# Eight images through a convolution–attention–experts block: the next image's first normalisation moved beside the experts, small products and evictions re-placed

## The reference, cut to what matters

```python
x  = group_norm(hidden, pre_g, pre_b) + pos_emb               # the "first normalisation"
sw = sigmoid(conv1x1(silu(conv3x3(silu(conv1x1(x))))))        # c1, c2, c3
sh = group_norm(x, norm_g, norm_b).transpose                  # tokens; q, k, v of 8 heads of 16
standard_out = softmax(q k^T / 4) v
multi_out = two 64-wide attentions, queries from (x * sw), keys and values from sh
x  = group_norm(ff(concat(standard_out, multi_out))) + hidden
t  = tokens(x)
t += attention(layernorm(t))                                  # 8 heads of 16
t += top-2-of-8 experts(layernorm(t))                         # 128 -> 512 -> 128, exact gelu
```

## Time and profile before

| | us |
|---|---|
| median of 3 runs (lowest, highest) | 3018.26 (3012.58, 3019.98) |
| profiled execution, its own time | 3020.56 |
| its span | 3018.8 |
| PE busy / DVE / ACT / POOL in the span | 2588.5 / 2057.8 / 1783.0 / 657.9 |
| mean granted TensorE clock | 0.95 of 2.4 GHz |
| one pass of the loop (first activation after the experts, L1313, 661.0 to 2769.8 for 7) | 351.5 |

### The profile page before, as it was taken

How to read it: one execution, slowest core, us unless ns; L and a number is a source line. 1 busy time by engine, 2 the same in 40 slices (tenths; PEclk the granted TensorE clock), 3 DMA queues, 4 the chain that set the end, 5 groups by cost and what they waited for, 6 DMA issues and landing times. The chain is left out here.

```text
span 3018.8 us, 42335 instructions
## 1 busy us (share of the span) xinstructions
PE 2588.5 (86%) x15054; PEld 1029.8 (34%) x15061; DVE 2057.8 (68%) x3120; ACT 1783.0 (59%) x3502; POOL 657.9 (22%) x611
## 2 busy tenths in 40 slices
PE   3796899988989899998999889898999989998844
PEld 1122222362225322262223522253222722235234
DVE  4756878477875878667785768758786677857520
ACT  1562577556765577556775567655775567755713
POOL 4000122015120240203320151202402043202123
PEclk9997899999999999999999989999999989999957
DMA  4002220274014530164202740145301632037034
GB/s 115 2 1 49 53 33 14 88 187 75 8 52 134 115 71 1 57 193 84 38 15 92 183 77 5 57 132 111 71 1 57 198 83 34 16 99 177 11 99 137
DMA packets 171978, 228.25 MB, mean 76 GB/s; under 512 B 29680, under 2 KB 101520, under 8 KB 171664
## 3 DMA queue, kind: packets, MB, share of 16 engines
q1 hardware_dynamic: 163600, 208.90, 28.4%
q0 software_dynamic: 8192, 16.79, 2.0%
HBM read 173.39 MB, written 51.31 MB: 74 GB/s over the span
## 5 line engine op out<-in xcount | busy, mean ns | idle before, releaser
L1433 DVE TENSOR_REDUCE blockmax<-ps 128x2 f32<-128x1024 f32 x1152 | 1355.0, 1220 | 380.1 <-PE ps L787 317.2
L1249 ACT ACTIVATE prob<-ps 128x512 f32<-128x512 f32 x2048 | 1110.7, 596 | 464.9 <-PE ps L964 453.2
L964 PE MATMUL ps<-qs,ks 99*128 99x512 bf16 x2048 | 687.2, 396 | 110.6 <-ACT prob L1249 48.5
L964 PEld LDWEIGHTS ps<-qs,ks 99*128 99x128 bf16 x2048 | 177.8, 99 | 775.0 <-ACT prob L1249 641.7
L624 POOL TENSOR_TENSOR rs<-vn,vec 128x1 f32<-128x1 f32 (+1 forms) x40 | 40.2, 1005 | 1475.1 <-DVE vn L1378 1051.2
L1297 ACT ACTIVATE prob<-ps,b1t 128x128 f32<-128x128 f32 x736 | 209.7, 368 | 169.3 <-PE ps L1080 169.3
L980 PE MATMUL ps<-prob,va_b 128*32 128x512 f32 x1984 | 283.8, 646 | 1.1 <-ACT oatt L1241 1.1
L980 PE MATMUL ps<-prob,va_a 128*32 128x512 f32 x2048 | 275.7, 610 | 3.0 <-ACT oatt L1241 1.7
L1275 ACT ACTIVATE prob<-ps 128x1024 f32<-128x1024 f32 x128 | 130.2, 1023 | 160.3 <-PE ps L1037 92.8
L675 POOL DMA_INDIRECT x_dram<-ta,slot_u x128 | 124.6, 973 | 313.5 <-DVE slot_u L1653 276.9
L1033 PE MATMUL ps<-routed,km 64*128 64x512 f32 x512 | 146.8, 651 | 12.6 <-DMA mrow<-maxrow 12.6
(11 more groups left out here) (247 smaller groups left out, 3182.6 us busy)
## 6 DMA issues: line engine op xcount, KB each, us to landing
parts_dram<-parts SPq DMA_DIRECT2D x32, 768.0 KB, 4.3
ks<-parts_dram SPq DMA_DIRECT2D x192, 128.0 KB, 4.4
qs<-parts_dram SPq DMA_DIRECT2D x384, 64.0 KB, 4.4
shared<-in_w SPq DMA_DIRECT2D x96, 256.0 KB, 3.4
prob<-in_w SPq DMA_DIRECT2D x96, 256.0 KB, 3.3
routed<-in_w SPq DMA_DIRECT2D x80, 256.0 KB, 3.5
xe<-in_w SPq DMA_DIRECT2D x48, 256.0 KB, 3.4
oatt<-in_w SPq DMA_DIRECT2D x48, 256.0 KB, 3.2
```

Of the source, the lines that this page charges most:

```text
L964: pe.matmul(ps[:, SC + h % 2, :], ks[:, slot_of(a, g), h, t * P:(t + 1) * P], qs[:, slot_of(a, g), q, h, :], start=True, stop=True).then_i ...
L1249: act.activation(prob[:, n % 3, h, :], ps[:, SC + h % 2, :], ACT.Exp, scale=HD ** -0.5).then_inc(exp_done[a], 1)
L1433: dve.tensor_reduce(cells, banks, AX.X, ALU.max).then_inc(blocks_used[f], 1)
```

## The change

- `pre` moves from token step 1 to expert slot 16, between pairs 5 and 6; `start_pre` to slot 8 on DVE; `load_next` from fetch 18 to fetch 11 on SP. x1 = ca * xin + cb is now made by ACT in halves in slots 18 and 19 (`scale_x`), and POOL adds the positions (`add_positions`).
- Token steps: start_x1 1 (was 3), start_x2 2 (5), norm 3 (6), start_xh 5 (7), normalisation in two halves at step 6 (8), kA0 6, kA1 7, qA0 8, qA1 9 (were 9, 10, 11, 13), vA 10, 11 (14, 15), vm 13, 14 (18, 19), c10 and c11 stay at 16, 17, c2 25 (24).
- ACT reads a small product of step n-1 in the middle of step n (between exponentials 1 and 2), in both windows, where it read that of step n at its end.
- The early pairs: one after `hidden`, one after `expert_out` in each slot from 13 on (were 1 in slot 13, 3 in slot 14, then 2 together behind `expert_out`).
- `third_part_b` moves from DVE to POOL; q's remainder goes to `tb`, so q no longer waits for k's third part. ACT's small products of a slot come before `second_part_b`.
- POOL's second reciprocal root stands behind 4 gathers instead of 12. On SP `spread_max("b", 2)` stands ahead of `spread_parts(0, 0)`.

```diff
-TOKEN_WINDOW = {1: ["pre"], 4: ["turn_b_1"], 6: ["norm"], 9: ["kA0"], 10: ["kA1"], 11: ["qA0"], 12: ["turn_b_2"],
-                13: ["qA1"], 14: ["vA0"], 15: ["vA1"], 16: ["c10"], 17: ["c11"], 18: ["vm0"], 19: ["vm1"],
-                20: ["turn_b_3"], 21: ["res0"], 22: ["res1"], 24: ["c2"], 26: ["c30"], 27: ["c31"],
+TOKEN_WINDOW = {3: ["norm"], 4: ["turn_b_1"], 6: ["kA0"], 7: ["kA1"], 8: ["qA0"], 9: ["qA1"], 10: ["vA0"],
+                11: ["vA1"], 12: ["turn_b_2"], 13: ["vm0"], 14: ["vm1"], 16: ["c10"], 17: ["c11"],
+                20: ["turn_b_3"], 21: ["res0"], 22: ["res1"], 25: ["c2"], 26: ["c30"], 27: ["c31"],
                 28: ["turn_a0_0"]}
-TOKEN_EXTRA = {0: ["start_pre"], 2: ["start_x0"], 3: ["start_x1"], 5: ["start_x2"], 7: ["start_xh"]}
+TOKEN_EXTRA = {1: ["start_x1"], 2: ["start_x2"], 5: ["start_xh"]}
-TURN_PAIR = UNIT
-BETWEEN_PAIRS = {2: "tg4", 9: "tg5", TURN_PAIR: "turn_b_0"}
+TURN_PAIR = UNIT + 1
+BETWEEN_PAIRS = {2: "tg4", 5: "pre", 8: "tg5", TURN_PAIR: "turn_b_0"}
+COEFS_PAIR = 8
+SCALE_SLOTS = (18, 19)
...
+def early_items(s, place):
+
+    d = SLOT_PAIRS * (s - PAIR_SLOT) + place
+    if s < PAIR_SLOT:
+        return []
+    return [x for x in (BETWEEN_PAIRS.get(d - 1), d) if x is not None]
...
-        rem = ta
+        rems = (ta, tb)
...
             if front:
+                if token:
+                    spread_max("b", 2)
                 spread_parts(0, 0)
                 spread_group(0, 0, 0)
-                if token:
-                    spread_max("b", 2)
...
-                        if token and front and (k, t) == (1, NT // 2):
+                        if token and front and (k, t) == (0, NT // 2):
                             rstd("norm_rstd", 1)
...
+            def add_positions():
+
+                for h in range(2):
+                    pool.wait_ge(done["x_scaled"], h + 1)
+                    pool.tensor_tensor(x1[:, cols(h)], x1[:, cols(h)], posw[:, cols(h)], ALU.add).then_inc(done["x1"], 1)
...
                     if experts and 1 <= s <= TILES:
                         hidden(s - 1)
+                    if token:
+                        for item in early_items(s, 0):
+                            early_item(item)
                     if experts and 2 <= s <= TILES + 1:
                         expert_out(s - 2)
...
+                    if token:
+                        for item in early_items(s, 1):
+                            early_item(item)
...
-                        exps(1, n)
+                        exps(1, n, 0)
+                    if token and front and n == 6:
+                        normalize(0)
+                    for name in small.token.get(n - 1, ()):
+                        small_product(name)
+                    if token:
+                        exps(1, n, 1)
+                    if token and front and n == 6:
+                        normalize(1)
...
-                    if i == 1:
-                        dve.wait_ge(done["k3_a"], h + 1)
-                    dve.tensor_tensor(rem[:, cols(h)], ps[:, SM, :], parts[:, i, 0, cols(h)], ALU.subtract
+                    dve.tensor_tensor(rems[i][:, cols(h)], ps[:, SM, :], parts[:, i, 0, cols(h)], ALU.subtract
...
+                        if s == 8 and front:
+                            start_pre()
+                        for item in early_items(s, 0) + early_items(s, 1):
+                            if item == BETWEEN_PAIRS[TURN_PAIR]:
+                                small_product(item)
+                            elif item == "pre" and front:
+                                small_product(item)
+                            elif item not in BETWEEN_PAIRS.values():
+                                reduce_pair("b", item, early_banks(item))
+                                if item == COEFS_PAIR and front:
+                                    scale_coefs()
```

More of the change, by code:

```diff
@@ L178, in without_front, with without_start @@
     return name.startswith(("turn_b", "res"))
+def without_start(name):
+    return name != "pre"
 def for_last_norm(name):
@@ L566, in sync_program @@
                         load_rows(4 + i // 16)
-                    if i == 18 and token and front:
+                    if i == 11 and token and front:
                         load_next()
@@ L685, in pool_program @@
                 keep_parts_b()
-                if experts and front:
+                if front:
                     rstd("pre_rstd", 1)
+                    add_positions()
                 if experts:
@@ L1241, in take_output, with exps @@
                 act.activation(oatt[:, f, :], ps[:, OB, :], ACT.Copy).then_inc(o_taken[a], 1)
-            def exps(a, n):
-                if n >= 3:
+            def exps(a, n, half):
+                if n >= 3 and half == 0:
                     act.wait_ge(pv_done[a], n - 2)
-                for h in range(GH):
+                for h in (2 * half, 2 * half + 1):
                     act.wait_ge(scores_ready[a], GH * n + h + 1)
@@ L1298, in scalar_program @@
                                            bias=b1t[:, i, c:c + 1]).then_inc(gelu_done, 1)
+                    if conv:
+                        for name in small.expert.get(s, ()):
+                            small_product(name)
                     if token:
@@ L1302, in scalar_program @@
                                 second_part_b(name)
-                    if conv:
-                        for name in small.expert.get(s, ()):
-                            small_product(name)
+                        if front and s in SCALE_SLOTS:
+                            scale_x(SCALE_SLOTS.index(s))
                 if not token:
@@ L1315, in scalar_program @@
                 if not token:
-                    normalize()
+                    for h in range(2):
+                        scale_x(h)
+                    normalize(0)
+                    normalize(1)
                 for n in range(2 * STEPS):
-                    if token and front and n == 8:
-                        normalize()
                     if token:
@@ L1331, in scalar_program @@
                             second_part(name)
-                    for name in small.token.get(n, ()):
-                        small_product(name)
         def vector_program(dve, conv, experts, token, front, small):
@@ L1493, in small_product @@
                 elif name == "start_x2":
-                    group_stats(x1, "norm", start=1)
+                    start_x2()
                 elif name == "start_xh":
@@ L1761, in vector_program @@
                 small_product("pre")
-                start_x0()
+                scale_coefs()
                 start_x1()
-                group_stats(x1, "norm", start=1)
+                start_x2()
                 small_product("norm")
@@ L1787, in build @@
         run_block(NB - 1, True, True, True, False,
-                  Windows(conv=CONV_WINDOW, parts=PARTS_WINDOW, expert=EXPERT_WINDOW,
+                  Windows(conv=CONV_WINDOW, parts=PARTS_WINDOW, expert=only(EXPERT_WINDOW, without_start),
                           token=only(TOKEN_WINDOW, without_front)))
```

99 lines of the change are left out of this document (50 added, 49 removed).

## The result

The changed kernel takes 2975.2 us (median of 4 runs, 2971.88 to 2982.73) beside 3019.1 (3012.58 to 3023.96) for the kernel before on the same chip: ratio 0.9859, 95% interval 0.9832 to 0.9887. It is 1.4% faster, by 44 us where 104 were forecast, and lies outside the range (2882 to 2962). One pass of the loop takes 345.3 us (351.5 before, 337 forecast).

What follows compares the result with a forecast made beforehand. No engine is full in the token window; PE and ACT handing over two score banks, plus waits, bound it. Gains of 1.9 + 11.5 + 1.2 = 14.6 us a full pass, 103.8 in all, gave 2914.5 us; range 2882 to 2962.

Steps and rivals of the forecast that it cites:

- the last image's block: Last image's block was said to have the expert stage and conv gains only: 3.5 us.
- Steps 0 to 12: Token window's start: 17.9 us for steps 0 to 5, then 5.4, 4.9, 3 x 3.85, 3.5 and 2.9.
- The stall of step 6: Token step 6: ACT still waits about 2.2 us for DVE's coefficients; step 5.4, next 4.1 plus 0.8 for the clock.
- the projections' 3.85: Token steps 7 to 10: PE waits 0.35 for a bank handed on late, 3.85 us each instead of 3.50.
- The largest term: Token window: about 6 us gained through the earlier start and normalisation, counted over steps through kA0 and step 7.
- Steps 13/14, "2 x 3.5": Token steps 13 and 14, with vm's projections: 3.5 us each.
- Rival E: POOL's added 6.9 us holds up DVE's pairs; a pass gains 7.7, 2962 us; chance 0.05.
- Step 16, "3.0 + 1.2": Token step 16: with turn 2's maxima first on SP, PE's wait and the cold step go, 3.0 + 1.2 us.
- cover 2 us: SP queue: next image's spread ends near 1440, ahead of turn 3's rows, landed 1444, wanted at step 24 at 1446.
- Mid-step eviction, "near nothing": ACT's mid-step reads: 12 us gained or 12 lost possible; -1.4 + 1.7 taken, near nothing.
- Rival D: Mid-step eviction becomes the chain: 29 steps lose 0.65 each, 4.3 a pass lost, about 3048 us; chance 0.05.
- The expert stage, 1.9: Expert stage: token step 0 starts at 1364.9, not 1366.79, 1.9 us gained (bounds 0 and 3.5); slot 15 1.4 earlier.

Runs made afterwards that it cites:

- all four together: Changed kernel with turn 3's rows first, coefficients a step earlier, token-window evictions at step's end, PSUM split for token turns 2 and 3 only: 2909.9 us.
- the earlier coefficients: Changed kernel with the second norm's coefficients computed behind step 4's turn instead of behind step 5's pairs; alone 2978.6 us.

## Why the prediction was wrong

The sign was right and so were most terms; the sum failed by 8.4 us a pass (6.2 gained where 14.6 were forecast). The token window is 9.7 us over the forecast: 0.7 up to step 13, 2.0 in step 14, 4.6 in steps 22 to 24, 1.0 in 25 and 26, 1.3 in 30. The other stages gained 1.4 more than forecast, for a reason that the forecast did not have (the expert stage, below). One sum of the forecast is also off by itself: the last image's block was given 3.5 us, where its two terms, 1.9 and 1.2, make 3.1.

- *Steps 0 to 12*: right within 0.7 us, in part because misses cancel: steps 0 to 6 take 1.7 us too long, 7 to 12 take 1.1 less than said. The stall of step 6 was called (5.4 and 4.9; measured 5.96 and 4.10), so were the projections' 3.85 (3.80). The largest term, about 6 us for the earlier normalisation, came out at 5.0 by its own reckoning (the waits over bare steps fall from 11.5 to 5.3, and step 7 keeps 1.2).
- *Steps 13/14, "2 x 3.5"*, and with them 22 and 30: the first failed step. The turn was costed at 1.2 us wherever it falls; beside POOL's combination it costs 3.0 and step 14 takes 5.49 (5.19 where the clock holds). The same hold is in step 22 (4.52, and 2.92 with the split in PSUM) and step 30 (4.36, and 3.00). Rival E had the mechanism and put it on the wrong instructions: the pairs do read PSUM and stayed at 4.62 for four, but the split's conversion and last subtraction do not. (The 1.23 that rival E compares with k's 2.18 is q's third part, of the same size.) The Trainium skill (SBUF — State Buffer, "SBUF: two separate sides") names two kinds of VectorE operation that a running GpSimd operation shuts out for its whole length: one in a two-port mode, and one with two SBUF inputs while the GpSimd operation reads SBUF. The prediction took only the second. The trace agrees with both: 2.13 us for a conversion that takes 0.21 alone, and 0.28 beside the same POOL operation when it reads PSUM; 1.34 for a subtraction of two SBUF operands that takes 0.28. That the conversion runs in a two-port mode no row shows directly.
- *Step 16, "3.0 + 1.2"*: the second failed step is its cover. The term itself was right (5.2 measured in the kernel before with that line alone). "It ends near 1440, ahead of turn 3's rows; cover 2 us" was wrong: measured from the first score, the train ended at 80.5 us and not at 75, the rows landed at 86.3 and not at 79, and were wanted at 83.8. The place of the train was carried over from the earlier trace rows by hand, not walked part by part. With the order changed, steps 23 and 24 are 2.9 us shorter.
- *Steps 26 and 30* (0.6 and 1.3 us over): with evictions at the step's end they take 3.83 and 3.08 again, the latter since turn a0_0's split (1.73) leaves POOL's way.
- *Mid-step eviction, "near nothing"*: a term of two signs. In the convolution window it gives 2.65 us a pass (108.10 against 110.75; 1.2 forecast), in the token window it costs 3.0 (119.11 against 116.14; 4.8 by the run with both windows' evictions at the end). Rival D's sign was real there; its size was a fifth of what it needed.
- *The expert stage, 1.9*: 1.2 measured in the quoted pass, from `hidden(12)`, slot 13's first product, to the first score (39.0 to 37.85). Slot 15 begins 1.6 us earlier behind `hidden(12)` (1.4 forecast); slots 15 to 24 then lose 0.4, where setting the pairs apart and the rest were to gain 0.5. But the quoted pass is one of two. In the other four full passes of the kernel before, slot 15's products run at the lower clock behind two waits for DVE's reductions, and the stage takes 40.6 us (PE before, the pass after the quoted one):
```profile
1686.94 0.65 PE L826 MATMUL ps<-wt,prob 128*128 128x128 f32 x4 [1.32 <-DVE blockmax L1433]
...
1688.39 1.69 PE L1080 MATMUL ps<-prob 128*128 128x128 f32 x8
1689.88 1.92 PE L1090 MATMUL ps<-prob 128*128 128x128 f32 x8
```
  After, that wait and the lower clock are gone in all passes, which the forecast had no term for. In the quoted pass and the one before it the lower clock stands at the end of the convolution window instead (its last value product takes 1.65). So parts and experts together take 121.9 us in five of the six full passes before (123.1 in the first, which has both) and 119.1 in all six after: 1.6 of these 2.8 us is a stretch at the lower clock.
- *Covers that held*: `start_pre` read its image at 1303.7, asked for at 1294.9 and landed at most 4.9 us later; POOL's gathers were in time.

Beside the two failed steps the interaction was missing. Each repair alone is worth between -16 and +26 us, 20 in all, and all four together 65. An open wait behind a mended one can hide the mending: with the PSUM split alone, step 23 grew by 1.4 us at turn 3's rows. That this holds for each of the four is not shown; every run with several repairs had the earlier coefficients in it. With all four the token window takes 109.65 us where the walk said 109.4, a pass 336 where it said 337, and the kernel 2909.9 where 2914.5 was said. That agreement is in part luck: it is another kernel than the one forecast, and its steps miss both ways (0 to 5 take 19.4 for 18.4, 6 and 7 take 8.4 for 10.3, step 13 takes 4.3 for 3.5).

## What to carry to other kernels

When a change moves a window in time, list what runs beside each short instruction of the other engines in its new place. A DVE conversion or a subtraction of two SBUF operands on a critical chain wants its operand in PSUM, if the bank can be spared for it, and should not start beside a long POOL operation. Walk the queue of SP part by part, too: a transfer moved ahead pushes the next train into what follows. Judge repairs of a chain of waits together: alone, two of the four here looked worthless or harmful. Look at every pass of a loop before one is quoted: 1.6 us of the expert stage's gain stand in four passes of six and not in the quoted one. And "mid-step of the next step" is later than "end of this one"; which of the two is right depends on the window.

## What the runs showed of the hardware

- A POOL addition of 128x1024 holds a DVE conversion of 16x128 from SBUF to SBUF until it ends (2.13 us; 0.21 alone); one of 32x512 holds a subtraction of two SBUF operands too (1.34 and 1.38; 0.28 alone). With the source in PSUM both take 278 ns in the mean of 72 (278 and 278), beside the same POOL operations; the price is 0.07 on the conversion and a bank held for 0.6 us more, which cost 0.6 us in each of steps 13 and 21.
- The same wait does not always bring the clock down, not even in one kernel. At the end of the convolution window PE waits 1.58 to 1.60 us in every full pass of the kernel before; the value product behind it takes 1.64 to 1.93 us in three of the six passes (mostly at 1.2 GHz) and 1.06 in the other three (2.4 GHz). In slot 15 the waits of 1.32 and 0.48 are followed by a hidden product of 1.16 in the two passes where that product had been the one at the lower level, and of 1.69 to 1.93 in the other four. A wait of 0.75 in the convolution window was followed by 1.80, two waits of 0.61 and 0.74 at step 14 by 1.06. Which it will be, no run here settled.
